# The fused last stage of a Flamingo block: TensorE runs values and scores together, turned integers go to the score banks, VectorE and ScalarE take their work in another order

## The chip, the core and the metric

The kernel runs on one core of one Trainium2 chip. The metric is the device time in microseconds (us). The core has TensorE (PE in the profile; PEld is its weight load), VectorE (DVE), ScalarE (ACT) and GpSimd (POOL) for computing, and SyncE (SP) for issuing transfers. They run side by side, each takes its own instructions in program order, and they wait for each other through semaphores. The matrix products land in PSUM, which this kernel divides into eight banks of 512 float32 values a partition; everything else lies in SBUF.

## The reference, cut to what matters

128 sequences of 64 tokens with 128 features pass through two layers, each a gated cross-attention and a gated feed-forward part. The change touches only the last stage, which computes the second layer:

```python
x = x + jnp.tanh(g_xattn[1]) * _L1_xattn_ref(_layernorm(x), ctx_1024, ctx_1024, mask, w_q, w_k, w_v, out_w, out_b)
x = x + jnp.tanh(g_ffn[1])   * _L1_ffn_ref(_layernorm(x), w1, conv_w, conv_b, w2)

# _L1_xattn_ref: 16 heads of 64
f = einsum('bhqd,bhkd->bhqk', fq, fk) / 8 + mask          # scores
ps = softmax(f)                                            # probabilities
attns = einsum('bhqk,bhkd->bhqd', ps, fv)                  # value product
return attns @ out_w.T + out_b

# _L1_ffn_ref: 512 hidden features
h = bit_linear(x, w1)          # x rounded to integers in -128..127 by a row's step, w1 to -1, 0, 1
h = depthwise_conv1d(h)        # three taps along the sequence, per feature
h = silu(h)
return bit_linear(h, w2)       # h rounded to integers too
```

## The kernel before, in words

The 8192 tokens are 64 tiles of 128 rows (two sequences each). `attention_ffn` is a software pipeline over turns `k` = 0 to 67, written out by hand: in each turn every engine does one piece of each of several tiles, at fixed distances. In turn `k` tile `k-1` has its keys, queries and scores computed, tile `k-2` its exponentials, values and normalisation, tile `k-4` its value product and output product. The feed-forward part follows in the same turn for older tiles: unit `k-11` of the hidden layer (a quarter of the 512 hidden features for a group of four tiles) and, for unit `k-12`, the SiLU; tile `k-16` is transposed back and its largest value found, tile `k-17` is rounded and multiplied by `w2`. After turn 67 a short tail finishes the last tiles.

What each engine does in a full turn, in order:

- TensorE (L1373 on): first half of the keys (`project_k`, L1248), first half of the probabilities transposed (`turn_probs`, L1283), the input transposed (`turn_x`, L1240), second half of the probabilities, second half of the keys, `hidden` (L1334), first half of the queries (`project_q`, L1256), the value product (`values`, L1297, 32 products of 64x64), second half of the queries, `turn_back` (L1363), the values (`project_v`, L1263), the `scores` (L1274, again 64x64), `project` (L1371), once in four turns `turn_xq` and `turn_steps` (L1317, L1326: a group's integers, and its steps along rows), `project_out` (L1305), `turn_h` (L1353).
- VectorE: statistics of the tile just finished (`new_stats`, L1706), `collect` of an expert result (L1573, L1576, L1579), `layernorm` (L1675), `scale` (L1714), `sums` (L1692) and `invert` (L1697) of the softmax, `conv_left` and `conv_right` (L1722, L1731), `twice_silu` (L1738), `residual` (L1758), `add_bias` (L1681), `tops` (L1688), `add_x` (L1702), `largest` (L1743), `scales`. Between them stand five slots of small operations, `small(k, 0)` to `small(k, 4)`: the 25 steps of a group's normalisation and rounding (`ffn_in`) are spread over three turns out of four (`k` mod 4 = 3, 0 and 1; none where it is 2), the 17 steps of the first normalisation (`norm1`) over three turns out of eight. They are 128x4 or 128x8 arithmetic, and in a few places 128x128 or 128x512.
- ScalarE copies PSUM to SBUF (`take_...`), takes the exponentials (`exps`, L1452), the middle tap (`centre`, L1483), the tanh (L1490) and the rounding (L1501).
- GpSimd works on the scores in SBUF: `shift` (L1824) subtracts a row's largest value after `tops`, `normalise` (L1829) multiplies by the inverse sum after `invert`; it also adds the output bias (`add_bo`, L1834) and issues the gathers of `yr` (L1839).

PSUM is shared out by name: banks S0 and S1 hold the scores, Y0 and Y1 keys, queries and values in turn, T0 and T1 probabilities and value product. Bank M holds `turn_x`, `turn_back`, the turned integers and `project_out`; bank F holds `hidden`, the turned steps, `turn_h` and `project`. `take_bank` makes TensorE wait until the last reader of M or F is done.

## Time and profile before

| | |
|---|---|
| median of 3 runs | 1615.91 us (1614.13 to 1621.37) |
| span of the profiled execution | 1602.7 us (the profile gives no other time for it) |
| median above the span | 13.2 us |
| TensorE busy | 1480.6 us (92%) |
| VectorE busy | 1177.7 us (73%) |
| ScalarE, GpSimd busy | 990.6 us (62%), 693.3 us (43%) |
| the fused stage: first and last turn's `turn_x` | 744.9 and 1526.1 us after the start |

The span is the time from the first to the last instruction of one profiled execution. A share of busy time is a mean over the whole program; the stage that is changed begins near 745 us, and is read by itself below. The rows show one line per group of instructions or per instruction: the engine, the line of the kernel, the operation, what it writes and reads, and how long it took. Turns are named by `k`.

### The profile page before, as it was taken

To read this page: it belongs to the slowest core of one execution; us is meant where nothing else is said; L and a number is where in the kernel's file an instruction comes from. 1 tells how busy PE (TensorE), PEld (TensorE's weight loads), DVE (VectorE), ACT (ScalarE), POOL (GpSimd) and SP (SyncE) were. 2 spreads that over 40 slices of the span, in tenths; PEclk is the share of its full clock that TensorE was granted. 3 is DMA by queue.
4 is the path that set the end of the run, shared out by engine and by line. 5 is a ranking of instruction groups with operands and counts; after the bars stand their busy time and mean duration, and the time that the engine had idled before them with its cause. 6 is when DMAs were issued, how large, how long until landed. Compare 5 with 4: busy or idle time off the path is not lost.

```text
span 1602.7 us, 51795 instructions
## 1 busy us (share of the span) xinstructions
PE 1480.6 (92%) x20229; PEld 1223.7 (76%) x20229; DVE 1177.7 (73%) x3089; ACT 990.6 (62%) x1990; POOL 693.3 (43%) x605
## 2 busy tenths in 40 slices
PE   4999999999559999996999999999999999999987
PEld 2777777777559999995778777887878777888864
DVE  5688888899623222234688999989999899988875
ACT  3687777876223444442566676666767766677756
POOL 2234666676711111144665545444544544333310
PEclk9799999998679999998999999999999999999999
DMA  9999970000166777761100000000000000000000
GB/s 291 399 388 384 373 248 25 25 32 25 52 222 210 231 229 225 233 187 37 32 24 19 19 19 23 24 23 22 22 22 26 22 22 22 12 12 12 14 9 24
DMA packets 95626, 169.90 MB, mean 106 GB/s; under 512 B 11984, under 2 KB 43728, under 8 KB 95152
## 3 DMA queue, kind: packets, MB, share of 16 engines
q1 hardware_dynamic: 82800, 140.35, 26.4%
q0 software_dynamic: 11600, 26.10, 4.9%
q8 instruction: 155, 2.54, 0.6%
q10 hardware_dynamic: 1008, 0.40, 0.1%
q14 instruction: 63, 0.52, 0.1%
HBM read 75.71 MB, written 91.10 MB: 104 GB/s over the span
## 4 chain that ended last, share of the span: by engine, by line
PE 26%; DVE 19%; issue 6%; ACT 2%; POOL 1%; DMA 1%; DVEq 0%; ACTq 0%
PE L1psY L1263 4%; PE L1psY L1256 4%; PE L1psM L1305 3%; PE L1psY L1248 3%; DVE L1sc L1681 2%; PE L1psS L1274 2%; PE L1psT L1297 2%; DVE L1den L1692 2%; DVE L1am L1743 1%; PE L1psT L1283 1%; DVE x L1573 1%; DVE L1psF L1714 1%; DVE L1hc L1722 1%; POOL yr L1839 1%; PE L1psF L1334 1%
## 5 line engine op out<-in xcount | busy, mean ns | idle before, releaser
L980 ACT ACTIVATE GhT<-GpsH,Gwx 128x256 f32<-128x256 f32 x284 | 118.6, 470 | 158.9 <-PE GpsH L948 157.5
L1436 ACT ACTIVATE L1KT<-L1psY 128x512 f32<-128x512 f32 x128 | 77.5, 606 | 221.9 <-PE L1psY L1248 220.3
L1824 POOL TENSOR_TENSOR L1sc<-L1sc,L1top 128x1024 f32<-128x1024 f32 x64 | 121.8, 1903 | 212.8 <-DVE L1top L1688 212.8
L1829 POOL TENSOR_TENSOR L1sc<-L1sc,L1rden 128x1024 f32<-128x1024 f32 x64 | 121.8, 1904 | 175.5 <-DVE L1rden L1697 175.5
L836 POOL TENSOR_TENSOR L0sc<-L0sc,L0top 128x1024 f32<-128x1024 f32 x64 | 121.6, 1900 | 159.0 <-DVE L0top L566 158.9
L996 DVE TENSOR_TENSOR yg<-GpsY,Gwx 128x256 f32<-128x256 f32 x71 | 30.1, 425 | 168.7 <-PE GpsY L956 168.4
L1248 PE MATMUL L1psY<-cx,L1WK 128*128 128x128 f32 x1024 | 137.5, 278 | 12.0 <-DVE L1identh L1764 12.0
L1256 PE MATMUL L1psY<-L1xnT,L1WQ 128*128 128x128 f32 x1024 | 142.4, 283 | 0.0
L956 PEld LDWEIGHTS GpsY<-Gwx,GhT 128*128 128x128 f32 x1136 | 137.6, 192 | 3.3
L842 POOL DMA_INDIRECT rows_in<-L0xr,slot x128 | 124.7, 974 | 34.0 <-issue 30.5
L1081 POOL DMA_DIRECT2D rows_out<-yg x71 | 38.9, 547 | 230.3 <-issue 230.3
L956 PE MATMUL GpsY<-Gwx,GhT 128*128 128x128 f32 x1136 | 138.2, 275 | 0.0
L1263 PE MATMUL L1psY<-L1WV,cx 128*64 128x512 f32 x512 | 127.6, 616 | 10.8 <-ACT L1QT L1441 10.6
L948 PE MATMUL GpsH<-GxT,Gwx 128*128 128x256 f32 x568 | 136.3, 384 | 0.0
L1248 PEld LDWEIGHTS L1psY<-cx,L1WK 128*128 128x128 f32 x1024 | 126.4, 194 | 12.3 <-DVE L1identh L1764 12.2
L1256 PEld LDWEIGHTS L1psY<-L1xnT,L1WQ 128*128 128x128 f32 x1024 | 126.2, 193 | 6.0 <-ACT L1xnT L1431 0.2
L1305 PE MATMUL L1psM<-L1WO,L1OT 128*128 128x128 f32 x1024 | 129.4, 280 | 0.7 <-ACT L1xiT L1469 0.7
L1839 POOL DMA_INDIRECT yr<-rows_out,slot x112 | 108.4, 968 | 34.3 <-issue 19.4
L1305 PEld LDWEIGHTS L1psM<-L1WO,L1OT 128*128 128x128 f32 x1024 | 120.6, 194 | 1.9 <-issue 1.1
L948 PEld LDWEIGHTS GpsH<-GxT,Gwx 128*128 128x128 f32 x568 | 103.8, 193 | 11.4 <-DVE GxT L990 0.2
L1274 PEld LDWEIGHTS L1psS<-L1KT,L1QT 64*64 64x64 f32 x4096 | 66.4, 136 | 52.5 <-issue 51.6
L327 PE MATMUL L0psS<-L0KT,L0QT 32*64 32x256 f32 x1024 | 89.3, 418 | 15.6 <-ACT L0V L464 7.3
(310 smaller groups left out, 3668.3 us busy)
## 6 DMA issues: line engine op xcount, KB each, us to landing
Gwx<-in_experts SPq DMA_DIRECT2D x71, 579.0 KB, 4.0
rows_in<-L0zero SPq DMA_DIRECT2D x1, 33792.0 KB, 93.1
rows_out<-L0zero SPq DMA_DIRECT2D x1, 33792.0 KB
Gxg<-rows_in SPq DMA_DIRECT2D x71, 128.0 KB, 3.5
rows_out<-yg POOLq DMA_DIRECT2D x71, 128.0 KB, 3.8
cx<-in_ctxT SPq DMA_DIRECT2D x64, 64.0 KB, 1.8
out<-X SPq DMA_DIRECT2D x64, 64.0 KB, 1.7
L0ctxT<-in_ctxT SPq DMA_DIRECT2D x1, 2560.0 KB, 18.9
```

Source lines behind the costliest of these rows:

```text
L836: nc.gpsimd.tensor_tensor(sc[:, t % 4, :, :], sc[:, t % 4, :, :], top[:, t % 2, :].unsqueeze(2).broadcast_to([P, H, S]), ALU.subtract).the ...
L842: nc.gpsimd.indirect_dma_start(xs, bass.IndirectOffsetOnAxis(ap=slot[:, t, k:k + 1].bitcast(U32), axis=0), xr[:, t % XR, :], None).then_in ...
L948: last = mm(psH[:, u, m, :], wx[:, w, m * P:(m + 1) * P], xT[:, u, :], start=True, stop=True)
L956: last = mm(psY[:, u, i, :], hT[:, u, m, i * P:(i + 1) * P], wx[:, w, o2 + m * D:o2 + (m + 1) * D], start=(m == 0), stop=(m == FM - 1))
L980: nc.scalar.activation(hT[:, u, m, :], psH[:, u, m, :], ACT.Gelu, bias=wx[:, w, ob1 + m:ob1 + m + 1]).then_inc(s["h_ready"], 1)
L1248: last = mm(psY[:, c, i * P:(i + 1) * P], WK[:, j * P:(j + 1) * P], cx[:, t % CR, :], start=True, stop=True)
L1256: last = mm(psY[:, c, i * P:(i + 1) * P], WQ[:, j * P:(j + 1) * P], xnT[:, t % 2, :], start=True, stop=True)
L1263: last = mm(psY[64 * p:64 * p + 64, b, :], cx[:, t % CR, 64 * b:64 * b + 64], rhs, start=True, stop=True)
L1305: last = mm(psM[:, 1, :], OT[:, t % 2, i, :], WO[:, i, :], start=(i == 0), stop=(i == HP - 1))
L1824: nc.gpsimd.tensor_tensor(sc[:, t % SR, :, :], sc[:, t % SR, :, :], broad(top[:, t % 2, :]), ALU.subtract).then_inc(s["shifted"], 1)
L1829: nc.gpsimd.tensor_tensor(sc[:, t % SR, :, :], sc[:, t % SR, :, :], broad(rden[:, t % 2, :]), ALU.mult).then_inc(s["probs_ready"], 1)
L1839: nc.gpsimd.indirect_dma_start(yr[:, t % YR, k, :], None, ys, bass.IndirectOffsetOnAxis(ap=slot[:, t, k:k + 1].bitcast(U32), axis=0)).then ...
```

## The change

Five things are altered, all in the fused stage.

1. TensorE's order in a turn: `turn_back` stands behind the first half of the queries, then the second half of the queries, then `values`, and `scores` right behind it, ahead of `project_v`.
2. The turned integers and steps are written to the score banks S0 and S1 instead of M and F. They are placed behind `project_out`; they wait for `scores_out` of the turn (that is `add_bias`), and the next `scores` wait until ScalarE has read them (`xqT_ready`, `steps_ready`).
3. `project_out` waits for the two halves of `OT` apart.
4. ScalarE: the first copy of the probabilities comes after `rounding` and `take_xnT`; both query copies come ahead of `exps`; `take_z` and `tanh` come ahead of the two copies `take_o`.
5. VectorE: `conv_left` and `conv_right` move from behind `invert` to ahead of `small(k, 2)` and `sums`; `add_bias` moves ahead of `residual`.

```diff
@@ bank
             if stage == "xq":
-                return ("M", psM[:, 2:4, :]) if t // G4 < INT_GROUPS else ("F", psF[:, :])
+                return ("S", flat(psS[:, 0, :, :])) if t // G4 < INT_GROUPS else ("F", psF[:, :])
+            if stage == "steps":
+                return "S", flat(psS[:, 1, :, :])
@@ scores
+                g = min((t + LX - FX - 1) // G4 + 1, INT_GROUPS)
+                wait(pe, s["xqT_ready"], g)
+                wait(pe, s["steps_ready"], g)
@@ project_out
-                pe.wait_ge(s["OT_ready"], 2 * t + 2)
                 for i in range(HP):
+                    if i % 4 == 0:
+                        pe.wait_ge(s["OT_ready"], 2 * t + i // 4 + 1)
@@ turn_xq, turn_steps
+                    pe.wait_ge(s["scores_out"], min(G4 * g + FX - LX + 1, NT))
...
-                take_bank("F", s["steps_ready"], g + 1)
+                ps = bank("steps", G4 * g)[1]
@@ TensorE's turn
                     project_q(tx, 0)
+                if tb is not None:
+                    turn_back(tb)
+                if tx is not None:
+                    project_q(tx, 1)
                 if tt is not None:
                     values(tt)
                 if tx is not None:
-                    project_q(tx, 1)
-                if tb is not None:
-                    turn_back(tb)
+                    scores(tx)
                 if tv is not None:
                     project_v(tv, 0)
                     project_v(tv, 1)
-                if tx is not None:
-                    scores(tx)
...
                 if tt is not None:
                     project_out(tt)
+                if k >= FX and (k - FX) % G4 == 0 and (k - FX) // G4 < INT_GROUPS:
+                    turn_xq((k - FX) // G4)
+                    turn_steps((k - FX) // G4)
@@ ScalarE's turn
-                if tt is not None:
-                    take_probs(tt, 0)
...
                     take_xnT(tx)
                 if tt is not None:
+                    take_probs(tt, 0)
                     take_probs(tt, 1)
...
-                if tv is not None:
-                    exps(tv)
                 if n is not None:
                     centre(n)
                 if tx is not None:
                     take_q(tx, 0)
+                    take_q(tx, 1)
+                if tv is not None:
+                    exps(tv)
+                if tb is not None:
+                    take_z(tb)
+                if n2 is not None:
+                    tanh(n2)
                 if tt is not None:
                     take_o(tt, 0)
...
                     take_o(tt, 1)
@@ VectorE's turn
                 small(k, 1)
+                if n is not None:
+                    conv_left(n)
+                    conv_right(n)
                 small(k, 2)
                 if tv is not None:
                     sums(tv)
                     invert(tv)
-                if n is not None:
-                    conv_left(n)
-                    conv_right(n)
                 small(k, 3)
                 if n2 is not None:
                     twice_silu(n2)
                 small(k, 4)
+                if tx is not None:
+                    add_bias(tx)
                 if tb is not None:
                     residual(tb)
                 if tx is not None:
-                    add_bias(tx)
                     tops(tx)
```

How the instructions stand on VectorE in a turn with `k` mod 4 = 0, from `scale` (L1714) to `tops` (L1688), before:

```order
L1714 TENSOR_TENSOR L1psF<-L1psF,L1step 128x512
L1600 SCALAR_TENSOR_TENSOR L1nv<-L1rstd 128x4
L1602 SCALAR_TENSOR_TENSOR L1nv<-L1nv 128x4
L1603 SCALAR_TENSOR_TENSOR L1rstd<-L1nv,L1rstd 128x4
L1600 SCALAR_TENSOR_TENSOR L1nv<-L1rstd 128x4
L1692 TENSOR_REDUCE L1den<-L1sc 128x16
L1697 RECIPROCAL L1rden<-L1den 128x16
L1722 SCALAR_TENSOR_TENSOR L1hc<-L1psF,F_taps,L1hc 128x8x63
L1731 SCALAR_TENSOR_TENSOR L1hc<-L1psF,F_taps,L1hc 128x8x63
L1602 SCALAR_TENSOR_TENSOR L1nv<-L1nv 128x4
L1603 SCALAR_TENSOR_TENSOR L1rstd<-L1nv,L1rstd 128x4
L1738 SCALAR_TENSOR_TENSOR L1hs<-L1hs,L1hc 128x512
```

The same stretch of VectorE in the changed kernel, whose line numbers are 6 higher (`conv_left` is L1728, `sums` L1698, `invert` L1703, `twice_silu` L1744):

```order
L1720 TENSOR_TENSOR L1psF<-L1psF,L1step 128x512
L1606 SCALAR_TENSOR_TENSOR L1nv<-L1rstd 128x4
L1608 SCALAR_TENSOR_TENSOR L1nv<-L1nv 128x4
L1728 SCALAR_TENSOR_TENSOR L1hc<-L1psF,F_taps,L1hc 128x8x63
L1737 SCALAR_TENSOR_TENSOR L1hc<-L1psF,F_taps,L1hc 128x8x63
L1609 SCALAR_TENSOR_TENSOR L1rstd<-L1nv,L1rstd 128x4
L1606 SCALAR_TENSOR_TENSOR L1nv<-L1rstd 128x4
L1698 TENSOR_REDUCE L1den<-L1sc 128x16
L1703 RECIPROCAL L1rden<-L1den 128x16
L1608 SCALAR_TENSOR_TENSOR L1nv<-L1nv 128x4
L1609 SCALAR_TENSOR_TENSOR L1rstd<-L1nv,L1rstd 128x4
L1744 SCALAR_TENSOR_TENSOR L1hs<-L1hs,L1hc 128x512
```

The two convolution taps stood between the reciprocal and the next small operations, and now stand between `scale` and the softmax sums; behind the reciprocal come the small operations and `twice_silu` at once.

TensorE in the middle of a turn, from `hidden` (L1334) to `project` (L1371), before:

```order
L1334 MATMUL L1psF<-L1xiT,F_W1b 128x512
L1256 MATMUL L1psY<-L1xnT,L1WQ 128x128 x4
L1297 MATMUL L1psT<-L1PT,L1V 64x64 x32
L1256 MATMUL L1psY<-L1xnT,L1WQ 128x128 x4
L1363 MATMUL L1psM<-L1identh,L1z 128x128 x4
L1263 MATMUL L1psY<-L1WV,cx 64x512 x4
L1274 MATMUL L1psS<-L1KT,L1QT 64x64 x32
L1371 MATMUL L1psF<-F_W,L1qT 128x128 x4
```

And TensorE there in the changed kernel, where the same calls have the lines 1342, 1258, 1371, 1258, 1302, 1279, 1265 and 1379:

```order
L1342 MATMUL L1psF<-L1xiT,F_W1b 128x512
L1258 MATMUL L1psY<-L1xnT,L1WQ 128x128 x4
L1371 MATMUL L1psM<-L1identh,L1z 128x128 x4
L1258 MATMUL L1psY<-L1xnT,L1WQ 128x128 x4
L1302 MATMUL L1psT<-L1PT,L1V 64x64 x32
L1279 MATMUL L1psS<-L1KT,L1QT 64x64 x32
L1265 MATMUL L1psY<-L1WV,cx 64x512 x4
L1379 MATMUL L1psF<-F_W,L1qT 128x128 x4
```

The two groups of 64x64 products now stand side by side, where 128x128 products and the 64x512 ones stood between them.

## Rows read from the trace of the kernel before

**Rows 1.** The page, part 1: busy us, share of the span, instructions.

```profile
PE 1480.6 (92%) x20229; PEld 1223.7 (76%) x20229; DVE 1177.7 (73%) x3089; ACT 990.6 (62%) x1990; POOL 693.3 (43%) x605
```

**Rows 2.** Busy time by stretch: stretch, length, engines' busy us, PE clock, DMA.

```profile
955.76:1365.10 409.34, 395.83 (x6658) 326.42 (x6657) 378.56 (x926) 285.71 (x529) 201.03 (x159) 1.00 0.08 23
1365.10:1526.10 161.00, 158.64 (x2704) 132.68 (x2703) 140.49 (x326) 114.63 (x215) 55.70 (x40) 1.00 0.05 13
```

**Rows 3.** Waits of VectorE and TensorE from 955.76 to 1365.1: total us, times, longest.

```profile
DVE X L1758 <- PE L1psF L1371: 9.9, 16, 1.1
DVE L1den L1692 <- ACT L1sc L1452: 2.4, 8, 0.4
DVE L1psF L1714 <- PE L1psF L1334: 2.2, 8, 0.3
DVE X L1702 <- PE L1psM L1305: 1.7, 8, 0.2
DVE L1hs L1738 <- ACT L1hs L1490: 1.2, 4, 0.3
...
PE L1psM L1240 <- DVE X L1702: 4.5, 8, 0.6
...
PE L1psF L1334 <- ACT L1z L1501: 2.6, 16, 0.2
```

**Rows 4.** VectorE in turn 44, in order of time: start us, us, instruction.

```profile
1275.82 0.72 DVE L1573 SCALAR_TENSOR_TENSOR x<-yr,weight,X 128x128 f32<-128x128 f32 x1
...
1277.69 0.69 DVE L1714 TENSOR_TENSOR L1psF<-L1psF,L1step 128x512 f32<-128x512 f32 x1
...
1278.48 0.16 DVE L1602 SCALAR_TENSOR_TENSOR L1nv<-L1nv 128x4 f32<-128x4 f32 x1
...
1280.19 0.25 DVE L1697 RECIPROCAL L1rden<-L1den 128x16 f32<-128x16 f32 x1
1280.37 0.65 DVE L1722 SCALAR_TENSOR_TENSOR L1hc<-L1psF,F_taps,L1hc 128x504 f32<-128x504 f32 x1
1281.05 0.74 DVE L1731 SCALAR_TENSOR_TENSOR L1hc<-L1psF,F_taps,L1hc 128x504 f32<-128x504 f32 x1
1281.71 0.74 DVE L1602 SCALAR_TENSOR_TENSOR L1nv<-L1nv 128x4 f32<-128x4 f32 x1
```

**Rows 5.** GpSimd in turn 44: `normalise`.

```profile
1280.53 1.90 POOL L1829 TENSOR_TENSOR L1sc<-L1sc,L1rden 128x1024 f32<-128x1024 f32 x1 [1.76 <-DVE L1rden L1697]
```

**Rows 6.** VectorE in turns 7 and 8, which have no convolution yet.

```profile
817.78 0.25 DVE L1697 RECIPROCAL L1rden<-L1den 128x16 f32<-128x16 f32 x1
...
818.15 1.88 DVE L1598 TENSOR_SCALAR L1rstd<-L1nv 128x4 int32<-128x4 int32 x1
...
828.88 2.63 DVE L1629 TENSOR_SCALAR L1xd<-X,L1mean 128x128 f32<-128x128 f32 x4
```

**Rows 7.** GpSimd in turn 7.

```profile
818.11 1.90 POOL L1829 TENSOR_TENSOR L1sc<-L1sc,L1rden 128x1024 f32<-128x1024 f32 x1 [1.34 <-DVE L1rden L1697]
```

**Rows 8.** ScalarE in turn 44.

```profile
1277.50 1.09 ACT L1452 ACTIVATE L1sc<-L1sc 128x1024 f32<-128x1024 f32 x1
1278.45 0.82 ACT L1483 ACTIVATE L1hc<-L1psF,F_bias,F_taps 128x512 f32<-128x512 f32 x1
1279.11 0.64 ACT L1441 ACTIVATE L1QT<-L1psY 128x512 f32<-128x512 f32 x1
1279.59 0.65 ACT L1462 ACTIVATE L1OT<-L1psT 128x512 f32<-128x512 f32 x1
```

**Rows 9.** TensorE in turn 44.

```profile
1276.87 1.05 PE L1256 MATMUL L1psY<-L1xnT,L1WQ 128*128 128x128 f32 x8
1277.85 1.16 PE L1297 MATMUL L1psT<-L1PT,L1V 64*64 64x64 f32 x64
1278.94 1.16 PE L1256 MATMUL L1psY<-L1xnT,L1WQ 128*128 128x128 f32 x8
1279.94 0.39 PE L1363 MATMUL L1psM<-L1identh,L1z 128*128 128x128 f16 x4
```

More of the change, by code:

```diff
@@ L1311, in turn_xq @@
                 name, ps = bank("xq", G4 * g)
-                take_bank(name, s["xqT_ready"], g + 1)
                 if g < INT_GROUPS:
+                    pe.wait_ge(s["scores_out"], min(G4 * g + FX - LX + 1, NT))
                     ps = halves(ps, BF16)
+                else:
+                    take_bank(name, s["xqT_ready"], g + 1)
                 x, eye = (xi, identb) if g < INT_GROUPS else (xq, ident)
@@ L1322, in turn_steps @@
                 pe.wait_ge(s["xq_ready"], g + 1)
-                take_bank("F", s["steps_ready"], g + 1)
+                ps = bank("steps", G4 * g)[1]
                 for i in range(G4):
                     t = G4 * g + i
-                    last = nc.tensor.transpose(psF[:, i * P:(i + 1) * P], inv[:, t:t + 1].broadcast_to([P, P]), ident[:])
+                    last = nc.tensor.transpose(ps[:, i * P:(i + 1) * P], inv[:, t:t + 1].broadcast_to([P, P]), ident[:])
                 last.then_inc(s["steps_ps"], 1)
@@ L1400, in _ @@
                     project_v(tv, 1)
-                if tx is not None:
-                    scores(tx)
                 if tb is not None:
                     project(tb)
-                if k >= FX and (k - FX) % G4 == 0 and k - FX < NT:
+                if k >= FX and (k - FX) % G4 == 0 and INT_GROUPS <= (k - FX) // G4 < NG:
                     turn_xq((k - FX) // G4)
-                if k >= FX and (k - FX) % G4 == 0 and (k - FX) // G4 < INT_GROUPS:
-                    turn_steps((k - FX) // G4)
                 if tt is not None:
                     project_out(tt)
+                if k >= FX and (k - FX) % G4 == 0 and (k - FX) // G4 < INT_GROUPS:
+                    turn_xq((k - FX) // G4)
+                    turn_steps((k - FX) // G4)
                 if th is not None:
@@ L1475, in take_steps @@
                 wait(act, s["h_scaled"], FM * (g - 1))
-                nc.scalar.activation(step[:, g % 2, :], psF[:, :], ACT.Copy).then_inc(s["steps_ready"], 1)
+                nc.scalar.activation(step[:, g % 2, :], bank("steps", G4 * g)[1], ACT.Copy).then_inc(s["steps_ready"], 1)
             def centre(n):
@@ L1531, in _ @@
                     take_q(tx, 0)
+                    take_q(tx, 1)
[5 more added lines that the diff above has]
+                    tanh(n2)
                 if tt is not None:
                     take_o(tt, 0)
-                if tx is not None:
-                    take_q(tx, 1)
-                if tt is not None:
                     take_o(tt, 1)
-                if n2 is not None:
-                    tanh(n2)
-                if tb is not None:
-                    take_z(tb)
                 if tv is not None:
```

## The prediction, before the changed kernel was run

> **What bounds the kernel now.** I read the shares first, then the fused stage alone, then its waits, then one turn of each engine. TensorE is busy 92% of the span and VectorE 73% [rows 1], which looks like a kernel bound by TensorE. In the stage that the change touches it is not so clear. From 955.76 to 1365.10 us lie 32 turns, so a turn takes 409.34 / 32 = 12.79 us; TensorE is busy 395.83 us of that and VectorE 378.56 us, 92% [rows 2]. The waits of VectorE there are 9.9 + 2.4 + 2.2 + 1.7 + 1.2 = 17.4 us, 0.54 a turn [rows 3]. What is left, 12.79 - 0.54 = 12.25 us, is what VectorE needs for a turn with the small gaps between its instructions; 11.83 of it is busy. In the next 161 us (13 turns of 12.38) it is busy 10.81 a turn, since the gathered expert results are all collected by then [rows 2]; with the same 0.42 of gaps it needs 11.2. TensorE in turn waits for VectorE at `turn_x`, 4.5 us [rows 3]. So two engines are near their limits, and VectorE, which has 12.25 us of work, can never let a turn fall much below that.
>
> How VectorE spends its turn matters most. In turn 44 the reciprocal starts at 1280.19, and GpSimd's `normalise` runs from 1280.53 to 1282.43 [rows 4, 5]. VectorE does the two convolution taps beneath it, 0.65 and 0.74 us; they read PSUM and pass unhindered. Then a 128x4 operation (L1602, at 1281.71) takes 0.74 us and ends at 1282.45, just behind GpSimd; the same line took 0.16 at 1278.48, with no GpSimd beside it [rows 4]. It was held until GpSimd's instruction was over. Turns 7 and 8 have no convolution, and show what happens when nothing stands there: L1598, 128x4 as well, is issued at 818.15 and takes 1.88 us, to 820.03, while `normalise` runs from 818.11 to 820.01 [rows 6, 7]; and four subtractions in turn 8 take 2.63 us together [rows 6]. At `collect` the same is seen beside `shift`: L1573 takes 0.72 us [rows 4].
>
> **The change part by part.** S is the start of `scale` in a turn.
>
> (a) *The taps leave the place beneath `normalise`.* Behind `invert` now come `small(k, 3)` and `twice_silu`. Where `k` mod 4 is 3, 0 or 1 an operation or two slip in ahead of GpSimd's start, 0.34 us after the reciprocal's [rows 4, 5], and the next is held to its end. With the taps in between, the held time was 0.74 - 0.16 = 0.58 us; without them it is 1.88 - 0.17 = 1.71 [rows 6]. That is 1.13 us more in three turns of four, 3.4 us in four turns. Where `k` mod 4 is 2 there is no small operation; `twice_silu` starts ahead of GpSimd and costs nothing more. Where `k` mod 4 is 0 or 1 the held operation is `twice_silu` itself, of which no row shows a full hold. The bounds are 0, if it passes as the taps do, and 1.71 [rows 4, 6]. I take 1.71: it takes two inputs from SBUF, as L1573 does, and that one is held [rows 4].
>
> The Trainium skill says it as a rule ("GPSIMD Engine Reference", section "Key points"): GpSimd shares its SBUF interfaces with VectorE, and contends with VectorE's instructions that have two SBUF inputs or run in a two-port mode. It would hold `twice_silu`, and let the taps pass, which the trace confirms for the taps (0.65 and 0.74 us beneath `normalise`). By the rule the term is 3.4 us in four turns; were only the small operations held, it would be 1.1.
>
> (b) *The taps now wait for ScalarE.* `conv_left` needs `centre`, and `centre` needs `scale`. `scale` lasts 0.69 [rows 4], `centre` 0.78 to 0.82 [rows 8], so with the two hand-overs `conv_left` can start at S + 1.55. VectorE has reached its place at S + 0.98 where two small operations stand in between (the second of them starts at 1278.48, S + 0.79, and takes its 0.19 to the next start [rows 4]), and at S + 0.60 where none do. Idle time: 0.55 in three turns of four, 0.95 in the fourth, 2.6 us in four turns. Before, `sums` and `invert` stood there and hid it.
>
> (c) *The sums wait for `exps`.* `exps` moves behind both query copies: S + 0.74 for `centre`, then 0.66, 0.48 and 0.48 to the starts of the two copies and of `exps`, and 1.09 for it, S + 3.45 [rows 8]. VectorE arrives after the taps (0.68 + 0.66) and two small operations at S + 3.28, or at S + 2.89 without them; where `k` mod 4 is 1, with more small work, later than `exps`. Idle: 0.17 + 0.17 + 0.56 + 0 = 0.9 us in four turns.
>
> (d) *`add_bias` ahead of `residual`, scores ahead of the values.* The scores stand in PSUM some 2 us earlier in TensorE's turn, and the wait of `residual` for `project` (9.9 us in 32 turns) goes. I take all of VectorE's waits as removed, 17.4 / 8 = 2.2 us in four turns. This is the most it can give.
>
> (e) *TensorE's order.* The two halves of the queries are the same eight instructions; the first lasts 1.05 us, the second, right behind the 64x64 products, 1.16 [rows 9]. So a change between shapes costs about 0.1, and the order before has five of them, the new one three: 0.2 us a turn. The wait of `hidden` for `rounding`, up to 0.2 us and 2.6 in 32 turns [rows 3], goes too, because `rounding` runs earlier on ScalarE. TensorE is busy 158.64 us in the 13 later turns [rows 2], 12.2 a turn; with this it needs about 11.8, of which some 0.15 is the group's integers and steps. All of this lies beside VectorE's 12.25 and more, and is worth nothing while VectorE is later. The bounds are 0 and, if TensorE alone set the time, 0.4 a turn.
>
> The Trainium skill's page "TensorEngine Tiling (Array Packing)", section "Key Properties", has the rule that a change of tiling mode drains the array. The rows agree with about 0.1 us each. By it alone the change would gain 64 x 0.2 = 13 us.
>
> (f) *Turned integers and steps in the score banks.* They wait for `add_bias` of the turn, which is over before `project_out` ends; their 0.67 us of TensorE work stays. The stall of `turn_steps` on `residual` goes, within (d). Where `k` mod 4 is 2 VectorE has no small operations and no hold, about 11.5 us by the terms above (its 12.25 less about 2.2 for a quarter's share of small work, plus 1.5 of (b) and (c)), and TensorE with the group's extra work needs about 12.0; it sets that turn, for 0.5 us more.
>
> (g) *Split wait for `OT`, ScalarE's other order at `take_z`, `tanh`, `take_o`:* ScalarE is busy 285.71 of 409.34 us [rows 2]; its copies come before TensorE asks for them, nothing either way, and 0.2 a turn at worst, hidden by VectorE's lateness.
>
> The sum for four turns: VectorE's need 4 x 12.25 = 49.0; plus 3.4, 2.6 and 0.9; plus 0.5 of (f): 56.4 us, against 51.2 before, so 14.1 for a turn instead of 12.79. Turns 11 to 50, 40 of them, give 40 x 1.3 = 52 us. In turns 51 to 64 it is (4 x 11.2 + 6.9) / 4 = 12.9 against 12.38: 14 x 0.5 = 7 us. In turns 1 to 10 there is nothing for (b); turns 7 and 8 hardly change, since no tap stood there; I count 0, with 4 us either way. The tail is untouched. Together +59 on the span of 1602.7, so 1662. The median of the runs lies 13.2 above the span, which gives 1675. Since (a) counts a full hold each time and (c) rests on tenths, I take 3 us off: 1672.
>
> **The rivals.**
>
> *Faster: VectorE's waits were the fault and nothing takes their place.* Then a turn falls to VectorE's 12.25, with TensorE at 11.8 below: 0.54 x 54 turns = 29 us, 1587; with the holds no longer than before this is the best case. For it speaks that 17.4 us of waits do go. Against it speaks that (a) needs only a small operation next to the reciprocal, and rows 6 show what that costs. It decides from the point where a held operation takes under 0.9 us.
>
> *Held for part of the time only.* `twice_silu` is not held, so (a) is 1.1, and (b) and (c) stay: 54.1 in four turns, +0.7 a turn, 28 + 3 us: 1647.
>
> *No change.* The small waits (b) and (c) vanish because `centre` and `exps` come earlier than I reckon, and only (a) stands: 49.0 + 3.4 = 52.4 against 51.2, but TensorE's earlier start gives back the rest: 54 turns of 0 to 0.1 us, 1616 to 1621.
>
> *Slower still, by TensorE's clock.* It was granted in full in both stretches [rows 2], with TensorE busy 96% and more. At 14.1 us a turn TensorE is idle for 2.4 of them. Should a tenth of the turns run at half clock, each would be some 11 us longer: 54 x 0.1 x 11 = 59 us more, 1731.
>
> **How the numbers follow.** The forecast has a chance of 0.70 (its own range 1650 to 1695), the part hold 0.13, no change 0.05, faster 0.08, the clock 0.04. What a measurement can tell from no change is about 0.5%, 8 us. The likeliest case gives 1672. The range from 1625 to 1698 leaves out the faster case, the clock and a little of each side. Faster 0.08, same 0.05, slower 0.87.
>
> **What would show it.** In the profile after, the small operations behind the reciprocal (L1604, L1609) and `twice_silu` (L1744) have instances of 1.8 to 2.3 us, and their means rise; `conv_left` (L1728) waits for ScalarE's `centre` some 0.5 us in every turn; `sums` wait for `exps`; VectorE's wait for `project` is gone; turns are near 14 us, save each fourth at 12; TensorE's waits are for VectorE (`turn_x`, and the bank of `turn_h`), and each group of 64x64 products has lost its edge. I am wrong if `twice_silu` stays at 0.77 us in the mean, if turns are under 12.8 us, or if VectorE's waits in the stage are below what they were.

## The result, and the profile after

The changed kernel took 1672.35 us in the median of four runs (1666.25 to 1684.05), the kernel before 1615.02 us in four runs on the same chip (1599.04 to 1621.37). The ratio on record is 1.040, 95% interval 1.035 to 1.045; the quotient of these two medians is 1.036, and the four runs of the kernel before lie 22 us apart. A second measurement on another chip (e6 below) gave 1.044 (1.038 to 1.051). The change makes the kernel slower. The profiled execution took 1675.47 us with a span of 1673.8 us; that of before had a span of 1602.7. The difference of the spans is 71.1 us; in the second measurement it was 70.7.

The page of the changed kernel, part 1, answers to [rows 1]; columns as there.

```profile
PE 1475.6 (88%) x20173; PEld 1232.8 (74%) x20229; DVE 1222.7 (73%) x3089; ACT 1001.7 (60%) x1990; POOL 707.0 (42%) x605
```

No engine received more instructions (TensorE's lower count is missing records), and VectorE's have 45 us more of busy time for the same 3089 instructions: something makes them longer. TensorE's share fell from 92 to 88%; it now waits.

Next the two stretches of 32 and 13 turns, answering to [rows 2]: stretch, length, busy us of TensorE, its weight loads, VectorE, ScalarE and GpSimd, then the granted clock of TensorE, DMA share and GB/s.

```profile
955.45:1405.60 450.15, 395.84 (x6627) 335.64 (x6658) 406.43 (x925) 290.44 (x529) 211.41 (x161) 0.98 0.08 21
1419.31:1593.97 174.66, 157.31 (x2692) 133.15 (x2704) 150.67 (x326) 117.90 (x215) 59.41 (x39) 1.00 0.04 12
```

A turn of the first is 450.15 / 32 = 14.07 us against 12.79, one of the second 174.66 / 13 = 13.44 against 12.38. TensorE has the same 395.84 us of work as before and is idle for the rest: 54.3 us instead of 13.5. VectorE is busy 28 us longer in the first stretch and idle 44 instead of 31. Both kinds of loss that the forecast spoke of are in these two numbers: longer instructions, and new idle time.

The waits of VectorE in the first stretch, answering to [rows 3]: who waits, for whom, total us, times, longest.

```profile
DVE L1hc L1728 <- ACT L1hc L1492: 19.8, 32, 0.8
DVE L1den L1698 <- ACT L1sc L1461: 5.0, 12, 0.5
DVE L1psF L1720 <- remote: 3.4, 5, 0.8
DVE L1am L1749 <- PE L1psF L1361: 3.2, 4, 0.8
...
DVE X L1764 <- PE L1psF L1379: 0.2, 1, 0.2
```

The wait of `residual` (L1764) for `project` is gone: 9.9 us, now 0.2. In its place `conv_left` (L1728) waits for `centre` in every one of the 32 turns, 19.8 us. In all VectorE's waits are 32.1 us where 17.4 stood.

The waits of TensorE there:

```profile
PE L1psF L1361 <- DVE X L1764: 40.3, 24, 2.3
PE L1psS L1279 <- issue: 4.6, 7, 1.2
PE L1psS L1279 <- ACT L1QT L1450: 4.5, 7, 0.9
PE L1psS L1325 <- DVE L1sc L1687: 2.8, 4, 0.7
```

TensorE's idle time is one wait: `turn_h` (L1361) needs the bank that `residual` (L1764) must empty first. Three turns of four it stands there, up to 2.3 us. TensorE runs behind VectorE. The second line is new: "issue" is a pause in the score products (L1279) that no semaphore explains. More on it below.

The rows of VectorE in turn 44, which answer to [rows 4]: start, us, instruction, and in brackets the idle time before it and what ended it.

```profile
1321.64 0.69 DVE L1720 TENSOR_TENSOR L1psF<-L1psF,L1step 128x512 f32<-128x512 f32 x1
...
1323.18 0.74 DVE L1728 SCALAR_TENSOR_TENSOR L1hc<-L1psF,F_taps,L1hc 128x504 f32<-128x504 f32 x1 [0.59 <-ACT L1hc L1492]
1323.96 0.74 DVE L1737 SCALAR_TENSOR_TENSOR L1hc<-L1psF,F_taps,L1hc 128x504 f32<-128x504 f32 x1
...
1325.10 1.22 DVE L1698 TENSOR_REDUCE L1den<-L1sc 128x16 f32<-128x1024 f32 x1
1326.35 0.25 DVE L1703 RECIPROCAL L1rden<-L1den 128x16 f32<-128x16 f32 x1
1326.52 0.10 DVE L1608 SCALAR_TENSOR_TENSOR L1nv<-L1nv 128x4 f32<-128x4 f32 x1
1326.66 0.16 DVE L1609 SCALAR_TENSOR_TENSOR L1rstd<-L1nv,L1rstd 128x4 f32<-128x4 f32 x1
1326.74 2.40 DVE L1744 SCALAR_TENSOR_TENSOR L1hs<-L1hs,L1hc 128x512 f32<-128x512 f32 x1
1329.07 1.07 DVE L1635 TENSOR_SCALAR L1xd<-X,L1mean 128x128 f32<-128x128 f32 x4
```

And GpSimd in that turn, answering to [rows 5]:

```profile
1326.69 1.91 POOL L1836 TENSOR_TENSOR L1sc<-L1sc,L1rden 128x1024 f32<-128x1024 f32 x1 [3.97 <-DVE L1rden L1703]
1328.56 0.90 POOL L1841 TENSOR_TENSOR X<-X,L1bo 128x128 f32<-128x128 f32 x1
```

Read the two together. S is 1321.64. The first tap starts at S + 1.54, after 0.59 us of idle time. Two small instructions behind the reciprocal slip in ahead of GpSimd's start at 1326.69, and `twice_silu`, issued at 1326.74, ends at 1329.14. GpSimd's instruction ends at 1328.60, and the usual 0.68 us of `twice_silu` fall almost wholly behind that point: it was held for 1.72 us. The hold works the other way too. GpSimd's `add_bo` is issued at 1328.56, while `twice_silu` is on its way, and takes 0.90 us; it takes 0.46 in e8 below, where only an instruction that reads PSUM stands beside it. It ends 0.32 us after `twice_silu`. The subtractions behind can't be the reason: they start at 1329.07, when a free `add_bo` would be over.

The same in the mean: `twice_silu` in the changed kernel, from 960 to 1400 us, with instructions, busy us, mean ns of one, and idle time before them,

```profile
L1744 DVE SCALAR_TENSOR_TENSOR L1hs<-L1hs,L1hc 128x512 f32<-128x512 f32 x31 | 53.5, 1724 | 0.0
```

and in the kernel before, from 952 to 1365 us:

```profile
L1738 DVE SCALAR_TENSOR_TENSOR L1hs<-L1hs,L1hc 128x512 f32<-128x512 f32 x32 | 24.7, 770 | 1.2 <-ACT L1hs L1490 1.2
```

That is 0.95 us more per turn from one line.

### The profile page after: what moved, and what is told of

It reads as the page before. It is cut to its first block, busy times and chain, and to the rows that moved or that the text cites. A ratio compares the mean times of both kernels' runs of the same rounds, so it can differ in the third digit from the quotient of the medians.

```text
span 1673.8 us, 51779 instructions
## 1 busy us (share of the span) xinstructions
PE 1475.6 (88%) x20173; PEld 1232.8 (74%) x20229; DVE 1222.7 (73%) x3089; ACT 1001.7 (60%) x1990; POOL 707.0 (42%) x605
## 4 chain that ended last, share of the span: by engine, by line
PE 24%; DVE 19%; issue 7%; ACT 3%; POOL 1%; DMA 1%; another core or an unknown queue 0%; DVEq 0%; ACTq 0%
PE L1psY L1258 5%; PE L1psY L1250 4%; PE L1psY L1265 3%; DVE L1sc L1687 3%; DVE L1den L1698 2%; PE L1psS L1279 2%; PE L1psT L1288 2%; PE L1psT L1302 2%; PE L1psM L1311 1%; DVE x L1579 1%; DVE L1top L1694 1%; PE L1psF L1361 1%; ACT L1sc L1461 1%; DVE L1psF L1720 1%; ACT L1hc L1492 1%
## 5 line engine op out<-in xcount | busy, mean ns | idle before, releaser
L1836 POOL TENSOR_TENSOR L1sc<-L1sc,L1rden 128x1024 f32<-128x1024 f32 x64 | 127.9, 1998 | 308.5 <-DVE L1rden L1703 308.5
L1250 PE MATMUL L1psY<-cx,L1WK 128*128 128x128 f32 x1024 | 142.1, 284 | 12.0 <-DVE L1identh L1770 12.0
L1250 PEld LDWEIGHTS L1psY<-cx,L1WK 128*128 128x128 f32 x1024 | 130.8, 200 | 13.0 <-DVE L1identh L1770 12.2
L842 POOL DMA_INDIRECT rows_in<-L0xr,slot x128 | 124.2, 971 | 33.5 <-issue 30.8
L1258 PEld LDWEIGHTS L1psY<-L1xnT,L1WQ 128*128 128x128 f32 x1024 | 130.0, 194 | 7.4 <-issue 4.7
L1279 PE MATMUL L1psS<-L1KT,L1QT 64*64 64x64 f32 x4096 | 78.8, 220 | 23.9 <-issue 13.6
```

What stands on the lines that cost most here:

```text
L842: nc.gpsimd.indirect_dma_start(xs, bass.IndirectOffsetOnAxis(ap=slot[:, t, k:k + 1].bitcast(U32), axis=0), xr[:, t % XR, :], None).then_in ...
L1250: last = mm(psY[:, c, i * P:(i + 1) * P], WK[:, j * P:(j + 1) * P], cx[:, t % CR, :], start=True, stop=True)
L1258: last = mm(psY[:, c, i * P:(i + 1) * P], WQ[:, j * P:(j + 1) * P], xnT[:, t % 2, :], start=True, stop=True)
L1279: last = mm(psS[q, p, j, :], QT[r, t % 2, j, q], KT[r, t % 2, j, q], start=True, stop=True)
L1836: nc.gpsimd.tensor_tensor(sc[:, t % SR, :, :], sc[:, t % SR, :, :], broad(rden[:, t % 2, :]), ALU.mult).then_inc(s["probs_ready"], 1)
```

## The experiments

A ratio is always against the kernel before on the same chip. The chips differ: on that of e1 to e4 the kernel before took 1665.12 us (18 runs), on that of e5 to e8 1605.12 (7 runs), on that of e9 to e12 1606.51 (11 runs). "Turn" is the mean of the 34 turns from 17 to 50, then that of the 13 from 51 to 63, by the starts of `turn_x`. For the kernel before they are 12.82 and 12.39, for the changed one 14.08 and 13.43; neither was traced on the chip of e1 to e4, so there the ratios decide, not the turns. A "pause" is a place inside a group of 64x64 products where two of them start more than 0.25 us apart. Its length is the distance of the two starts, about 0.2 us more than the idle time that the profile shows.

### e1: VectorE's old order in the changed kernel

```
@@ VectorE, a turn
                 small(k, 1)
-                conv_left(n); conv_right(n)
                 small(k, 2)
                 sums(tv); invert(tv)
+                conv_left(n); conv_right(n)
                 small(k, 3)
                 twice_silu(n2)
                 small(k, 4)
-                add_bias(tx)
                 residual(tb)
-                tops(tx)
+                add_bias(tx); tops(tx)
```

> The changed kernel with VectorE's old order (taps behind invert, residual ahead of add_bias); TensorE and ScalarE stay changed. My theory: the hold behind invert shrinks to 0.6 us and the wait for centre goes, but the sums now stand at S + 1.4 us and exps ends at S + 3.45, so VectorE waits 1.5 to 2.9 us a turn for exps, 8.4 us in four turns: turns of 14.3 us, about 1690 us, no better than the changed kernel. Rival (VectorE's new order alone is at fault): at or below 1616 us.

Measured: 1730.00 us, ratio 1.043 (1.035 to 1.050), turns 14.34 and 13.90. The waits of VectorE from 960 to 1400 us:

```profile
DVE L1den L1698 <- ACT L1sc L1461: 63.9, 31, 2.8
```

`exps` stands so late on ScalarE that `sums` wait for it 2 us in every turn. Restoring VectorE's order alone is no cure, because ScalarE's new order then costs as much by another way. (That VectorE's new order is costly by itself as well is seen in e12.) The early taps of the changed kernel fill the time in which `sums` would wait.

### e2: the same, with `exps` ahead of `centre`

```
@@ ScalarE, a turn (on top of e1)
                 take_k(tx, 1)
+                exps(tv)
                 centre(n)
                 take_q(tx, 0); take_q(tx, 1)
-                exps(tv)
```

> As the run before, and exps ahead of centre on ScalarE, so that only TensorE's new order, the score banks and the rest of ScalarE's order remain of the change. My theory: VectorE is back at the 12.25 us of work a turn that it needed before, its waits for project are mostly gone, TensorE needs 11.8: turns of 12.3, about 1590 us (1580 to 1603), faster than the kernel before by 1 to 2%. Rival (TensorE's or the banks' part costs something by itself): 1616 us or more.

Measured: 1649.19 us, ratio 0.992 (0.988 to 0.996), turns 12.97 and 12.69. With both orders back, what stays of the change (TensorE's order, the score banks, the split wait and the rest of ScalarE's order) is worth something, though less than the 0.984 expected. TensorE waits 11.4 us for the query copies (33 times from 950 to 1370 us) and pauses 21 times, 13.7 us, in the whole run.

### e3 and e12: the taps' place alone, in the kernel before

```
@@ VectorE, a turn (kernel before)
                 small(k, 1)
+                conv_left(n); conv_right(n)
                 small(k, 2)
                 sums(tv); invert(tv)
-                conv_left(n); conv_right(n)
                 small(k, 3)
```

> The kernel before with one edit, the two taps moved ahead of small(k, 2) and sums. My theory: longer holds behind invert, 3.4 us in four turns, and the wait for centre, 2.6: VectorE 13.75 us a turn, about 1655 us (1640 to 1670). Rival (the taps' place hardly matters, exps' place does): under 1625 us.

Measured: 1730.89 us, ratio 1.043 (1.036 to 1.051), turns 14.31 and 13.81. There were 55 pauses in the 64x64 products, 33.5 us, so on this chip it could not be told whether the taps or the pauses made it so slow. It was run again on a chip where the kernel before has no pause:

> The run e3 again (the kernel before with the two taps moved ahead of small(k, 2) and sums), on another chip if it falls so. There its ratio was 1.043, above the 1.024 that I had reckoned, and TensorE paused 55 times inside its 64x64 groups, 33.5 us. My theory: on a chip where the kernel before does not pause this one does not either, and the ratio is 1.025 to 1.035. Rival (the taps' place costs all of the change's 4% by itself): 1.040 or more without any pause.

Measured: 1681.86 us, ratio 1.047 (1.042 to 1.052), turns 14.13 and 13.81, and not one pause. The expectation fell: moving two instructions of VectorE costs as much as the whole change. Its waits from 960 to 1400 us, VectorE first:

```profile
DVE L1hc L1722 <- ACT L1hc L1483: 25.1, 31, 1.3
DVE X L1758 <- PE L1psF L1371: 3.8, 4, 1.0
```

and those of TensorE:

```profile
PE L1psF L1353 <- DVE X L1758: 21.1, 23, 1.6
PE L1psM L1240 <- DVE X L1702: 14.3, 23, 0.6
PE L1psY L1256 <- ACT L1xnT L1431: 10.9, 31, 0.4
PE L1psF L1326 <- DVE X L1758: 7.4, 8, 1.5
```

In this order of ScalarE `exps` precedes `centre`, so the taps wait for it up to 1.3 us instead of 0.8, 25.1 us in 31 turns; and the old wait of `residual` for `project` is not wholly gone (3.8 us). I had put into the expectation only the holds and the smaller wait. The other parts of the change give a little back at most: the full change stands at 1.040 and 1.044, the taps alone at 1.043 and 1.047, and the intervals overlap.

### e4: other cover beneath `normalise`

```
@@ VectorE, a turn (changed kernel)
                 sums(tv); invert(tv)
+                add_bias(tx); residual(tb)
                 small(k, 3)
                 twice_silu(n2)
                 small(k, 4)
-                add_bias(tx); residual(tb)
                 tops(tx)
```

> The changed kernel with add_bias and residual, which read PSUM, put directly behind invert, ahead of small(k, 3) and twice_silu. My theory: 1.5 us of VectorE's work runs beneath normalise again, each hold shrinks from 1.7 to about 0.5 us, and now in all four kinds of turn: 2.9 us less in four turns, 13.4 us a turn, about 1633 us (1620 to 1645). Rival (the holds are not the cost, the waits for centre and exps are): within 5 us of 1672.

Measured: 1665.46 us, ratio 1.003 (0.999 to 1.006), turns 13.11 and 12.67. The taps stay where the change put them; `add_bias` (1.21 us), which reads PSUM, now stands beneath GpSimd. The line of `twice_silu`:

```profile
L1744 DVE SCALAR_TENSOR_TENSOR L1hs<-L1hs,L1hc 128x512 f32<-128x512 f32 x31 | 24.3, 784 | 0.0
```

Its mean (from 960 to 1360 us) falls from 1724 to 784 ns, and the loss against the kernel before is gone, though the wait for `centre` is still there. The hold is not gone but short again: in turn 40 L1608 takes 0.69 us there. The edit also frees the bank of `turn_h` earlier, since `residual` is no longer behind the held instruction; so e4 shows what the whole chain costs (hold, `residual`, `turn_h`), and does not part it.

### e5 and e6: the two kernels once more, on one chip

> The kernel before, unchanged, one look on the chip of the next runs. In the four runs before this the times of the kernel before were 50 us higher than in the first trace, and in the traces of those runs TensorE paused inside its 64x64 groups shortly after a 16 KB transfer of the instruction queue, 21 to 55 times. My theory: where a chip's instruction transfers are slow the kernel before pauses too, and its fused stage takes 12.9 to 13.2 us a turn; on a chip like the first one it has no pause and 12.8. Rival (the other stages alone are slower): 12.8 us a turn and no pause, whatever the chip.

> The changed kernel, unchanged, for a ratio on this chip. My theory: VectorE sets its turn, so its ratio is near the first one, 1.03 to 1.045. Rival (part of the first ratio was the chip): under 1.02.

No edits. e5, the kernel before: 1603.99 us, span 1602.3, turns 12.81 and 12.39, no pause. e6, the changed kernel: 1678.41 us, ratio 1.044 (1.038 to 1.051), turns 14.02 and 13.42, 17 pauses of 16.1 us. So on these chips turns and pauses repeat from run to run; e3 and e12 show that the pauses can differ between chips.

### e7: half the dose

```
@@ GpSimd (changed kernel)
             def normalise(t):
-                tensor_tensor(sc[:, t % SR, :, :], sc[:, t % SR, :, :], broad(rden[:, t % 2, :]), mult)
+                tensor_tensor(sc[:, t % SR, 0:H // 2, :], sc[:, t % SR, 0:H // 2, :], (rden of those heads), mult)
```

Heads 8 to 15 are left undivided.

> The changed kernel, with normalise on heads 0 to 7 only; heads 8 to 15 of the probabilities are left undivided. GpSimd's instruction shrinks from 1.9 to about 0.95 us. My theory: each hold of VectorE shrinks by as much, in three turns of four, 0.71 us a turn over 58 turns, 38 to 41 us less than the changed kernel in the same runs, a ratio of about 1.015. Rival (VectorE is not held by the instruction, it waits for something else at that place): the time of the changed kernel within 5 us.

Measured: 1628.03 us, ratio 1.013 (1.007 to 1.018), turns 13.22 and 12.83. That is 50 us less than e6, where 38 to 41 were expected. Lines of e7 from 960 to 1350 us:

```profile
L1744 DVE SCALAR_TENSOR_TENSOR L1hs<-L1hs,L1hc 128x512 f32<-128x512 f32 x29 | 35.0, 1205 | 0.0
L1836 POOL TENSOR_TENSOR L1sc<-L1sc,L1rden 128x512 f32<-128x512 f32 x29 | 33.4, 1153 | 129.3 <-DVE L1rden L1703 129.3
```

and in turn 44:

```profile
1297.07 1.54 DVE L1744 SCALAR_TENSOR_TENSOR L1hs<-L1hs,L1hc 128x512 f32<-128x512 f32 x1
1297.01 1.05 POOL L1836 TENSOR_TENSOR L1sc<-L1sc,L1rden 128x512 f32<-128x512 f32 x1 [3.97 <-DVE L1rden L1703]
```

In turn 44 of the changed kernel the two took 2.40 and 1.91 us. GpSimd's instruction is 0.86 us shorter, and `twice_silu`, an instruction of another engine that was not touched, is 0.86 us shorter too. (The means fall by less for `twice_silu`, 0.52 us, because it is not the held one in every turn.) VectorE's order, its waits for `centre` and TensorE's order are as in the changed kernel. Of 73 us of loss (1678.41 - 1605.12), 50 go. The probabilities are ready earlier too, which this run cannot part from the hold; but seven turns of eight carry a hold (see (a) below), 0.86 x 7 / 8 = 0.75 us a turn, and the turns from 17 to 50 are 0.80 us shorter than those of e6.

### e8: everything read from the trace put together

```
@@ ScalarE (changed kernel)
+                exps(tv)
                 centre(n)
                 take_q(tx, 0); take_q(tx, 1)
-                exps(tv)
@@ VectorE
                 small(k, 1)
-                conv_left(n); conv_right(n)
                 small(k, 2)
                 sums(tv); invert(tv)
+                conv_left(n); conv_right(n)
+                add_bias(tx)
                 small(k, 3)
                 twice_silu(n2)
                 small(k, 4)
-                add_bias(tx)
                 residual(tb)
```

> The changed kernel with exps ahead of centre, the taps back behind invert, and add_bias directly behind the taps, ahead of small(k, 3) and twice_silu. My theory: 1.3 us of taps and 0.6 us of add_bias fill normalise, nothing is held behind invert, nothing waits for centre: VectorE needs 11.8 us a turn, TensorE 12.1: turns of 12.1 to 12.3, 2 to 3% faster than the kernel before, a ratio of 0.97 to 0.98. Rival (the score copies arrive too late for add_bias there, and TensorE's pauses decide): 0.99 to 1.00, no better than the run with exps early.

Measured: 1589.56 us, ratio 0.990 (0.984 to 0.996), turns 12.45 and 12.36. Faster than the kernel before, less than expected. VectorE in turn 44 of e8:

```profile
1267.20 0.25 DVE L1703 RECIPROCAL L1rden<-L1den 128x16 f32<-128x16 f32 x1
1267.37 0.65 DVE L1728 SCALAR_TENSOR_TENSOR L1hc<-L1psF,F_taps,L1hc 128x504 f32<-128x504 f32 x1
1268.06 0.74 DVE L1737 SCALAR_TENSOR_TENSOR L1hc<-L1psF,F_taps,L1hc 128x504 f32<-128x504 f32 x1
1269.62 1.22 DVE L1687 TENSOR_TENSOR L1sc<-L1psS,L1bias 128x1024 f32<-128x1024 f32 x1 [0.82 <-PE L1psS L1279]
...
1271.03 0.68 DVE L1744 SCALAR_TENSOR_TENSOR L1hs<-L1hs,L1hc 128x512 f32<-128x512 f32 x1
```

GpSimd in that turn:

```profile
1267.54 1.90 POOL L1836 TENSOR_TENSOR L1sc<-L1sc,L1rden 128x1024 f32<-128x1024 f32 x1 [2.61 <-DVE L1rden L1703]
1269.39 0.46 POOL L1841 TENSOR_TENSOR X<-X,L1bo 128x128 f32<-128x128 f32 x1
```

`twice_silu` has its 0.68 us. While `normalise` ran, VectorE did the taps and then, in this turn, waited 0.82 us for TensorE; in most turns `add_bias` follows the taps at once. Nothing was held. TensorE sets the turn again. Its waits in e8, 960 to 1350 us, show the next thing in its way:

```profile
PE L1psS L1279 <- ACT L1QT L1450: 9.5, 31, 0.5
PE L1psS L1279 <- issue: 1.8, 4, 0.7
```

### e9, e10, e11: the two waits of TensorE in e8

```
@@ e9, TensorE (on top of e8)
                 values(tt)
+                project_v(tv, 0)
                 scores(tx)
-                project_v(tv, 0)
                 project_v(tv, 1)
@@ e10, ScalarE (on top of e8)
                 exps(tv)
-                centre(n)
                 take_q(tx, 0); take_q(tx, 1)
+                centre(n)
@@ e11: both
```

> The run e8 with one edit on TensorE: the first half of the values between the value product and the scores, so that the two groups of 64x64 products stand apart again. In e8 TensorE still pauses 10 times inside the scores, 5.5 us together, and waits 0.3 us a turn for the second query copy ahead of them. My theory (the pauses come from instructions being taken faster than the 16 KB transfers bring them): no pause is left; the 0.85 us of values cover the wait for the copy, and two more changes of shape cost 0.2 us a turn. Together 5 us and 54 x 0.1 us less than e8, about 0.985 to 0.99 as a ratio. Rival (the pauses have another cause than the side-by-side groups): as many pauses as in e8, and a ratio of 0.99 or more.

> The run e8 with one edit on ScalarE: both query copies ahead of centre, behind exps. My theory: TensorE sets the turn in e8, and its wait of 0.3 us for the second query copy goes; centre comes 0.9 us later, and the taps wait up to 0.25 us, which VectorE has to spare: 0.25 us a turn over 54 turns, 13 us less than e8, a ratio near 0.982. Rival (VectorE sets the turn, and its taps come late): as e8 or slower, 0.99 to 1.0.

> The edits of e9 and e10 together on e8. My theory: no pause, no wait for the copy, but the two changes of shape stay: between e9 and e10, 0.98 to 0.985. Rival: the gains add up, 0.975 or less.

Measured: e9 1585.85 us, ratio 0.986 (0.981 to 0.990), turns 12.38 and 12.18, one pause of 0.3 us. e10 1581.49 us, 0.984 (0.980 to 0.988), turns 12.31 and 12.17, 17 pauses of 16.8 us. e11 1584.59 us, 0.985 (0.981 to 0.990), turns 12.37 and 12.18, one pause of 0.4 us. The three can't be told apart. All beat both kernels; e10 has the lowest median, 25 us below the kernel before on its chip; against the changed kernel the ratios put it 5 to 6% lower (0.984 to 1.040 and 1.044).

TensorE in e10, with the two groups of 64x64 products side by side and the scores' operands ready in time:

```profile
1256.53 1.16 PE L1302 MATMUL L1psT<-L1PT,L1V 64*64 64x64 f32 x64
1257.52 0.65 PE L1279 MATMUL L1psS<-L1KT,L1QT 64*64 64x64 f32 x28
1259.69 0.80 PE L1279 MATMUL L1psS<-L1KT,L1QT 64*64 64x64 f32 x36 [1.52 <-issue]
```

The query copies first remove the wait on them and put pauses in its place, 17 of some 1 us each where e8 had 10 of 0.55; separating the groups (e9) removes all pauses but one and pays for two more changes of shape. From the value product to the end of the values the groups' starts lie 4.20 us apart in e9 (1.09 + 1.01 + 1.09 + 1.01, medians) and 3.95 in e8 without its wait (0.99, taken from the changed kernel, + 1.09 + 1.87). That fits with e11 being no better than either, but no run parts the two.

## Why the prediction was right, and where it was not

The forecast was 1672 and the ratio it implies 1672 / 1616 = 1.035; measured were 1672.35 and 1.040. The direction and the mechanism are as forecast. That the two times agree so closely is partly luck: the span grew by 71 us, not by the 59 reckoned, and the 13.2 us that I put on top as the distance of a run's time to its span are really 1.7 (1675.47 against 1673.8; in e5 1603.99 against 1602.3). The profiled execution of before was simply a low one among its runs. Two errors of some 12 us cancelled. The four runs of before were high, too: the medians differ by 57.3 us here and by 73.3 in the second measurement, while the spans differ by 71.1 and 70.7.

Where the 71.1 us went, by the starts of `turn_x` in both traces:

| turns | before, us | after, us | more | reckoned |
|---|---|---|---|---|
| ahead of the stage | 744.9 | 743.5 | -1.4 | 0 |
| 1 to 10 | 112.3 | 115.0 | 2.7 | 0 |
| 11 to 16 | 72.2 | 82.1 | 9.9 | 7.8 |
| 17 to 50 | 435.7 | 478.6 | 42.9 | 44.2 |
| 51 to 63 | 161.0 | 174.7 | 13.7 | 7 |
| from 64 on | 76.5 | 79.8 | 3.3 | 0 |

(a) *The hold.* Right. It was taken at 1.71 us for `twice_silu`, from a small operation's hold and against a lower bound of 0; measured is 2.40 - 0.68 = 1.72. e7 shows that its length follows GpSimd's instruction, e4 that it is short again, and e8 that it goes, when PSUM work stands there. Not seen was that every second of the turns with `k` mod 4 = 2 is held too. They have a 128x8 operation of another norm behind the reciprocal; in turn 46 it takes 1.87 us, at 1357.99, where the same line took 0.16 at 1352.93. It stands behind `twice_silu` there, which had started ahead of GpSimd. So 7 turns of 8 carry a hold, not 6, on `twice_silu` or on a small operation (1.87 to 1.88 us): 7 x 1.13 / 2 = 4.0 us in four turns, not 3.4. Nor does `twice_silu` cost nothing where it starts first: `normalise` is then the held one and takes 2.29 us in turn 46 instead of 1.90.

The rule of the Trainium skill that the forecast weighed ("GPSIMD Engine Reference", section "Key points") is borne out with its consequence for `twice_silu`: two SBUF inputs, held; the taps and `add_bias`, one operand in PSUM, not held. L1604 has one SBUF input and is held as well, 1.88 us in turn 47; whether the rule's other condition, a two-port mode, covers it, no row shows.

(b) *The taps' wait for `centre`.* 2.6 us in four turns reckoned, 19.8 / 8 = 2.5 measured. Right; its arithmetic (S + 1.55) is met at S + 1.54.

(c) *The sums' wait for `exps`.* 0.9 reckoned, 5.0 / 8 = 0.6 measured. In turn 44 no wait is left, since the taps take 0.74 each and not 0.68 and 0.66.

(d) *Waits removed.* The 9.9 us of `residual` did go. But VectorE still waits for TensorE in places (3.4 + 3.2 us): I took all 17.4 us as removed, and 6.6 came back.

(e) *TensorE's shorter turn* was to be worth nothing while VectorE is late. Right: TensorE waits 40.3 us for VectorE in the changed kernel. With VectorE not late, e8 to e11 have turns of 12.3 to 12.45 instead of 12.8; VectorE's order differs there too, so that gain is not TensorE's alone.

(f) *The group turn* was to be set by TensorE at 12.0 us. Wrong: by the starts of `turn_x` the four kinds of turn (number mod 4 = 0, 1, 2, 3) take 14.5, 15.0, 13.4 and 13.4 us, where they took 12.3, 13.4, 13.3 and 12.1. TensorE's starts spread VectorE's lateness over the turns, so the starts of `scale` are the better measure: by them the kind `k` mod 4 = 2 takes 12.9 us, 12.5 where it has no hold and 13.4 where it has one. Nothing shows the 0.5 us of this term.

The sum can be checked on VectorE's own row, for four turns. Its busy time grew from 378.56 / 8 = 47.3 to 406.43 / 8 = 50.8 us, 3.5 more; its waits from 17.4 / 8 = 2.2 to 32.1 / 8 = 4.0, 1.8 more; the small gaps fell by 0.2. That is 51.2 + 5.1 = 56.3, as the trace has it. The forecast had 3.4 for the busy time, 1.3 for the waits (2.6 + 0.9 - 2.2) and 0.5 for (f), 56.4. So the sum is met because what (d) took away too freely about equals what (f) put on without need.

(g) *Nothing* was reckoned for it, and no run takes it alone. e3 and e12 show only that all parts other than the taps' place together move this kernel by a few us.

*The mis-sized step* is the sum for turns 51 to 63: 12.9 reckoned, 13.43 measured, 6.7 us over 13 turns. VectorE's waits were put at (2.6 + 0.9) / 4 = 0.9 us a turn and are 20.4 / 13 = 1.6. I had added the new costs to VectorE's need (11.2) and assumed that VectorE never waits for TensorE. The waits of VectorE there:

```profile
DVE L1hc L1728 <- ACT L1hc L1492: 8.9, 13, 1.0
DVE L1psF L1720 <- remote: 5.5, 10, 0.9
DVE L1den L1698 <- ACT L1sc L1461: 4.4, 10, 0.7
DVE L1am L1749 <- PE L1psF L1361: 1.6, 2, 0.8
```

`scale` (L1720) waits in 10 of 13 turns. It closes a loop: `twice_silu` is held, `residual` behind it empties its bank late, `turn_h` waits for the bank, the next keys and `hidden` stand behind `turn_h` on TensorE, and `scale` needs `hidden`. If, with less work of VectorE's own, this loop over both engines is longer than VectorE's row, adding up one engine's instructions can't see it. That reading is argued from the order and the waits, and not shown; e4, which takes `residual` out from behind the hold, is in keeping with it (12.67 there) but changes the hold too.

*The rivals.* "Faster" was to decide at a hold under 0.9 us; it was 1.72. "Held in part" falls with the 1724 ns of `twice_silu`. "No change" falls with the waits for `centre`. The clock did fall, but for less time than that rival needs: five stretches of 3.4 us at the lower of its two levels, 17 of 450 us, granted 0.98 in the mean, where the kernel before has none there. 0.02 x 450 is 9 us of TensorE's time at most, beside 54 us in which it is idle. How much of the 9 reached the end is not parted.

*Open.* How much of the 50 us in e7 is hold and how much earlier probabilities, beyond the 0.75 of 0.80 us a turn reckoned there. And why one chip takes 1665 us for the kernel that takes 1606 on others: some 30 us of it lie ahead of the fused stage, which begins at 767 to 778 us in the traces of e1 to e4 instead of 744.

## What to carry to other kernels

Before moving an instruction away from a place, ask what it shields there: find in the trace what runs on GpSimd at that moment, and which instruction will now be issued beneath it; one with two SBUF inputs is held to GpSimd's end, one that reads PSUM is not, and one that starts first holds GpSimd. A wait removed on one engine is worth nothing until the row of each engine it touches is written out again in its new order, with its hand-overs. And where two engines are within some per cent of each other, reckon the loop through both, not one engine's sum.

## What the runs showed of the hardware

- The hold is sharp, and runs to the end of GpSimd's instruction: 1.88 us for a 0.17 us instruction, 2.40 for a 0.68 us one, beside 1.90 to 1.91 us of GpSimd; with GpSimd's work halved (1.05 us), 1.54 for the second. It works the other way too, for the one that starts later: a 0.46 us addition of GpSimd took 0.90 beside `twice_silu`, and `normalise` 2.29 instead of 1.90.
- TensorE pauses in mid-group, and no semaphore explains it. Where the two groups of 64x64 products stand side by side, the changed kernel has 17 pauses inside the scores, 17.3 us in all from start to start, 13.6 us of it idle, 0.3 to 1.3 us each; the kernel before had none (e5). Each begins within 2.1 us of the start of a 16 KB transfer on the instruction queue: one begins at 1323.16 and lasts 1.45 us, and TensorE stops at 1324.85 until 1326.06, 1.21 us. TensorE's rows in turn 44, answering to [rows 9]:

```profile
1322.12 1.13 PE L1258 MATMUL L1psY<-L1xnT,L1WQ 128*128 128x128 f32 x8
1323.18 1.16 PE L1302 MATMUL L1psT<-L1PT,L1V 64*64 64x64 f32 x64
1324.17 0.68 PE L1279 MATMUL L1psS<-L1KT,L1QT 64*64 64x64 f32 x28
1326.06 0.80 PE L1279 MATMUL L1psS<-L1KT,L1QT 64*64 64x64 f32 x36 [1.21 <-issue]
...
1331.67 0.63 PE L1361 MATMUL L1psF<-ident,L1hs 128*128 128x128 f32 x4 [0.78 <-DVE X L1764]
```

  The pause costs nothing here, since TensorE waits for `residual` at the end of the turn anyway. One other group between the two (e9, e11) leaves one pause of 0.3 to 0.4 us. That short instructions are used up faster than they are brought fits these runs, but is not shown, and it can't be all: the very same kernel (e3, e12) had 55 pauses on one chip and none on another, 48 of the 55 in the value product, which had no 64x64 group beside it, and only 26 of them with such a transfer begun within them or at most 2.1 us ahead.
- A change of shape between groups of products costs TensorE about 0.1 us: the group behind the value product starts 1.09 us after it in the kernel before, where 128x128 products follow, and 0.99 us in the changed one, where the scores follow in the same shape (medians from 960 to 1400 us). The forecast had the same figure from [rows 9] on weaker ground: the second half of the queries still takes 1.13 us where no 64x64 group stands ahead of it.
